# A vision transformer tower: q and k stacks of 128 rows with zeros, a shared tile for W1 and the k stack, and another interleaving of the two image streams

## What is computed

```
h = x_patches @ W + b, class token ahead, + position            # tokens, (64, 197, 192)
h = h + attention(norm(h))     # layer 0: one head of width 192
h = h + ffn(norm(h))           # layer 0: per image ONE of 3 experts, 192 -> 768 -> 192, gelu, scaled by its score
h = h + attention(norm(h))     # layer 1: 12 heads of width 16, scale 1/4, then a projection
h = h + ffn(norm(h))           # layer 1: 192 -> 768 -> 192 for the 191 tokens past the first six; the first six
                               # go through a routed pair of small networks, at the end of the kernel
```

## Time and profile before

| | |
|---|---|
| median of three runs | 4402.16 us (4379.66 to 4405.91) |
| profiled execution | 4418.51 us, span 4416.7 us |
| PE busy | 3398.2 us, 77%, 23190 matmuls |
| DVE busy | 2136.5 us, 48% |
| ACT busy | 1404.5 us, 32% |
| POOL busy | 361.6 us, 8% |
| mean granted TensorE clock | 0.805 of full speed |
| DMA | 284.55 MB, mean 64 GB/s |

### The profile page before, as it was taken

How to read it: one execution, slowest core, us unless ns; L and a number is a source line. 1 busy time by engine, 2 the same in 40 slices (tenths; PEclk the granted TensorE clock), 3 DMA queues, 4 the chain that set the end, 5 groups by cost and what they waited for, 6 DMA issues and landing times.

```text
span 4416.7 us, 63033 instructions
## 1 busy us (share of the span) xinstructions
PE 3398.2 (77%) x23190; PEld 3035.2 (69%) x23190; DVE 2136.5 (48%) x5286; ACT 1404.5 (32%) x2904; POOL 361.6 (8%) x746
## 2 busy tenths in 40 slices
PE   5778777777787777887777877777778777787767
PEld 4767776677776676776666777667677666677655
DVE  4454454545454445455444445444545545544433
ACT  2333333233333333333233333323333323233321
POOL 1010000000010001000001000000000000100000
PEclk8778888778887788787777787877888878778778
DMA  4332322233222233222233232223322223322222
GB/s 116 74 75 64 75 64 52 47 74 71 68 65 55 44 75 74 64 70 50 47 72 74 64 75 64 50 50 74 74 66 68 52 44 75 74 64 65 54 40 54
DMA packets 101366, 284.55 MB, mean 64 GB/s; under 512 B 24183, under 2 KB 65416, under 8 KB 90317
## 3 DMA queue, kind: packets, MB, share of 16 engines
q1 hardware_dynamic: 101324, 283.99, 28.3%
HBM read 189.87 MB, written 15.00 MB: 46 GB/s over the span
## 4 chain that ended last, share of the span: by engine, by line
PE 54%; DVE 22%; DMA 8%; issue 8%; ACT 3%; POOL 2%; SPq 1%; DVEq 0%; POOLq 0%; ACTq 0%
PE banks L634 24%; PE banks L678 10%; PE banks L777 6%; DMA stack<-low 6%; PE banks L810 4%; PE banks L796 4%; DVE inv L1052 4%; DVE hx L946 4%; PE banks L658 2%; DVE nmax L1041 2%; DVE stats L934 2%; DVE xnT L972 2%; POOL rstd L580 2%; DMA stack<-nmaxT 2%; ACT xnT L1182 1%
## 5 line engine op out<-in xcount | busy, mean ns | idle before, releaser
L777 PE MATMUL banks<-stack 64*99 64x198 f32 x1536 | 326.2, 383 | 325.9 <-issue 187.7
L777 PEld LDWEIGHTS banks<-stack 64*99 64x99 f32 x1536 | 270.6, 273 | 378.6 <-issue 208.3
L1041 DVE TENSOR_REDUCE nmax<-banks 99x4 f32<-99x788 f32 x384 | 358.1, 975 | 289.4 <-PE banks L777 289.4
L634 PE MATMUL banks<-xnT,fc_wT 128*128 128x198 f32 x1920 | 442.3, 419 | 42.1 <-DVE xnT L972 42.1
L634 PEld LDWEIGHTS banks<-xnT,fc_wT 128*128 128x128 f32 x1920 | 415.8, 328 | 60.9 <-DVE xnT L972 51.3
L1182 ACT ACTIVATE xnT<-banks 128x396 fp32r<-128x396 f32 x192 | 96.2, 501 | 946.9 <-PE banks L658 946.9
L796 PE MATMUL banks<-stack 65*99 65x198 f32 x1536 | 284.5, 316 | 120.0 <-DMA stack<-nmaxT 98.2
L578 POOL TENSOR_TENSOR var_eps<-moments,eps 99x2 f32<-99x2 f32 x256 | 51.6, 201 | 3890.3 <-DVE moments L939 3890.3
L678 PE MATMUL banks<-w_sb,hidT 128*99 128x192 f32 x1536 | 351.1, 394 | 0.0
L796 PEld LDWEIGHTS banks<-stack 65*99 65x99 f32 x1536 | 223.6, 212 | 178.1 <-issue 127.0
L946 DVE TENSOR_SCALAR hx<-hx,moments,rstd 99x192 f32<-99x192 f32 (+1 forms) x768 | 247.3, 384 | 161.4 <-POOL rstd L580 157.7
(11 more groups left out here) (188 smaller groups left out, 5453.9 us busy)
## 6 DMA issues: line engine op xcount, KB each, us to landing
w_sb<-w_split SPq DMA_DIRECT2D x64, 1536.0 KB
xin<-in_x_dram SPq DMA_DIRECT2D x32, 1176.0 KB
w_sb<-in_L_ffn_W_dram SPq DMA_DIRECT2D x64, 576.0 KB, 6.7
stack<-hi SPq DMA_DIRECT2D x64, 297.0 KB, 4.9
stack<-hi SPq DMA_DIRECT2D x128, 148.5 KB, 6.0
stack<-low SPq DMA_DIRECT2D x128, 148.5 KB, 7.0
stack<-low SPq DMA_DIRECT2D x64, 297.0 KB, 8.8
out_dram<-y SPq DMA_DIRECT2D x64, 73.5 KB
```

The source lines that it names most:

```text
L634: last = t_.matmul(dst, a, b, start=(j == 0), stop=(j == len(pairs) - 1))
L777: last = t_.matmul(b[n % 4][0:R, t * SP_:(t + 1) * SP_], stack[p][0:SLOT, block_of(n, 0), t * R:(t + 1) * R], stack[p][0:SLOT, block_of(n, ...
L1041: v.tensor_reduce(nmax1[p][:, :, 4 * j:4 * j + 2].rearrange("p t h -> p h t"), src, AX, ALU.max, negate=True).then_inc(nmax1_ready[p], 1)
```

## The change

Three things.

**128 rows.** The stack of one tile is split into `q_stack` and `k_stack`, 128 partitions each and twelve head blocks in natural order. The matmuls of `max` and `att` now take all 128 rows. Rows 64 to 127 of `q_stack` are set to zero once, at the start; the rows of `k_stack` hold whatever W1 left there, and meet zeros. Row 64 of `q_stack` gets the maxima in each image, so it is zeroed again by a small copy before the next image's `max` stages. The copies into the stacks are four for q, at qk1_0, and four for k, at qk1_1, instead of six at qk1_1; the maxima are placed by two copies.

**Places.** `q_stack` has a place of its own. The first three quarters of W1 and a little of the fourth share a tile (`shared`) with `k_stack`; W1's last quarter is a tile `w1_last`, which shares its place with `headT`. W1 is loaded in two pieces. To make room, the set-up that splits W1 into parts has two staging buffers instead of three.

**Order.** `MERGE` is another string.

```diff
-STAGED = 3
+STAGED = 2
-MERGE = ("bbbbbabbabbbbabbababbbabaababbbababaaabbaaabababararbaabrbabbbaabrbbarabbrbaaaaa"
-         "aaabaababaaaabaababaaabaaabbabbrabbabaabbab")
+MERGE = ("abababbbabbaaabbbbaababbababbbbaabbbbaaabaabrrabbraarbbbbaabbbraaaabbaabarababab"
+         "aaabaababaaabaaaaababrbaabbabbabbaabababbab")
...
+        q_stack = [sb(f"q_stack{p}", [128, HEADS, SP_], F32R) for p in range(2)]
...
-                    w1_sb.append(sb(f"w1_sb{p}", [128, 2, 2, F], F32R, weights))
-                stack.append(sb(f"stack{p}", [SLOT + 1, 2 * HEADS, SP_], F32R, loop))
+                w1_sb.append(shared[p][:, 0:3 * F].rearrange("p (a f) -> p a f", a=3))
+                k_stack.append(shared[p][:].rearrange("p (h s) -> p h s", h=HEADS))
+                with ExitStack() as heads:
+                    headT.append(sb(f"headT{p}", [128, GROUPS, SP_], stack=heads))
+                w1_last.append(sb(f"w1_last{p}", [128, F], F32R, loop))
...
-                if name == "qk1_1":
-                    sp.wait_ge(hi_ready[p], 2 * it + 2)
-                    q, k = slice(0, 2 * SP_), slice(2 * SP_, 4 * SP_)
...
-                    sp.dma_start(slots[p][0:HD], high).then_inc(stacked[p], 16)
-                    sp.dma_start(slots[p][HD:2 * HD, :, k], high[:, k]).then_inc(stacked[p], 16)
-                    sp.dma_start(slots[p][2 * HD:3 * HD, :, q], high[:, q]).then_inc(stacked[p], 16)
-                    sp.wait_ge(low_ready[p], 2 * it + 2)
-                    sp.dma_start(slots[p][HD:2 * HD, :, q], rest[:, q]).then_inc(stacked[p], 16)
-                    sp.dma_start(slots[p][2 * HD:3 * HD, :, k], rest[:, k]).then_inc(stacked[p], 16)
-                    sp.dma_start(slots[p][3 * HD:SLOT], rest).then_inc(stacked[p], 16)
+                if name in ("qk1_0", "qk1_1"):
+                    j = int(name[4])
+                    part = slice(2 * SP_ * j, 2 * SP_ * (j + 1))
...
+                    dst = (q_slots, k_slots)[j][p]
...
+                    sp.wait_ge(hi_ready[p], 2 * it + 1 + j)
+                    sp.dma_start(dst[0:HD], high).then_inc(stacked[p], 16)
+                    sp.dma_start(dst[(2 - j) * HD:(3 - j) * HD], high).then_inc(stacked[p], 16)
+                    if j == 0:
+                        sp.dma_start(q_stack[p][SLOT:SLOT + 1].bitcast(F32), q_stack[p][128 - HEADS:, 0, :].bitcast(F32)).then_inc(stacked[p], 16)
+                    sp.wait_ge(low_ready[p], 2 * it + 1 + j)
+                    sp.dma_start(dst[(1 + j) * HD:(2 + j) * HD], rest).then_inc(stacked[p], 16)
+                    sp.dma_start(dst[3 * HD:SLOT], rest).then_inc(stacked[p], 16)
                 if name == "maxT":
                     sp.wait_ge(nmaxT_ready[p], it + 1)
-                    sp.dma_start(stack[p][SLOT:SLOT + 1].bitcast(F32), nmaxT[p][:].bitcast(F32)).then_inc(nmax_placed[p], 16)
+                    sp.dma_start(q_stack[p][SLOT:SLOT + 1].bitcast(F32), nmaxT[p][0:HEADS].bitcast(F32)).then_inc(nmax_placed[p], 16)
+                    sp.dma_start(k_stack[p][SLOT:SLOT + 1].bitcast(F32), nmaxT[p][HEADS:].bitcast(F32)).then_inc(nmax_placed[p], 16)
...
-                                             stack[p][0:SLOT, block_of(n, 0), t * R:(t + 1) * R],
-                                             stack[p][0:SLOT, block_of(n, 1), :], start=True, stop=True)
+                                             q_stack[p][:, n, t * R:(t + 1) * R], k_stack[p][:, n, :], start=True, stop=True)
...
-                                             stack[p][:, block_of(s, 1), kt * R:(kt + 1) * R],
-                                             stack[p][:, block_of(s, 0), :], start=True, stop=True)
+                                             k_stack[p][:, s, kt * R:(kt + 1) * R], q_stack[p][:, s, :], start=True, stop=True)
...
+                v.memset(q_stack[p][SLOT:].bitcast(F32), 0.0)
```

More of the change, by code:

```diff
@@ L167, in two @@
                 return [sb(f"{name}{p}", shape, dt, stack) for p in range(2)]
-            w1_sb, stack = [], []
+            w1_sb, w1_last, k_stack, headT = [], [], [], []
+            shared = two("shared", [128, HEADS * SP_], F32R)
             for p in range(2):
-                with ExitStack() as weights:
-                    w1_sb.append(sb(f"w1_sb{p}", [128, 2, 2, F], F32R, weights))
-                stack.append(sb(f"stack{p}", [SLOT + 1, 2 * HEADS, SP_], F32R, loop))
-            slots = [stack[p][:].bitcast(F32).rearrange("k (h e) s -> k h (e s)", e=4) for p in range(2)]
+                w1_sb.append(shared[p][:, 0:3 * F].rearrange("p (a f) -> p a f", a=3))
[3 more added lines that the diff above has]
+                w1_last.append(sb(f"w1_last{p}", [128, F], F32R, loop))
+            k_slots, q_slots = [[s[p][:].bitcast(F32).rearrange("k (h e) s -> k h (e s)", e=2) for p in range(2)]
+                                for s in (k_stack, q_stack)]
             w2_sb = two("w2_sb", [128, HC, D])
@@ L227, in vit_kernel @@
             turned = [probs[p][0][:, 1, :, :] for p in range(2)]
-            headT = two("headT", [128, GROUPS, SP_])
             y = two("y", [R, T, D])
@@ L749, in stages @@
                     if name == "hid0_0":
-                        pe.wait_ge(w1_loaded[p], 48 * it + 48)
-                    hidden(p, 0, int(name[5]), w1_sb[p], lambda c: slice(c * 128, (c + 1) * 128))
+                        pe.wait_ge(w1_loaded[p], 64 * it + 64)
+                    hidden(p, 0, int(name[5]), lambda c: lambda part, k: w1_row(p, 2 * part + k)[:, c * 128:(c + 1) * 128])
                 elif name[:4] == "out0":
@@ L821, in stages @@
                     pe.wait_ge(xnT_ready[p], norm_count(4, it))
-                    hidden(p, 1, int(name[5]), fc1_wT, lambda c: slice(c * 128, (c + 1) * 128))
+                    hidden(p, 1, int(name[5]), lambda c: columns(fc1_wT, slice(c * 128, (c + 1) * 128)))
                 elif name[:4] == "out1":
@@ L875, in _ @@
             for p in range(2):
+                v.memset(q_stack[p][SLOT:].bitcast(F32), 0.0)
+            for p in range(2):
                 v.memset(probs0[p][:, :, SEQ:SP_], 0.0)
@@ L1040, in stages @@
                     src = banks[p][0:R, k:k + 2, 0:T * SP_].rearrange("p h (t s) -> p h t s", s=SP_)[:, :, :, 0:SEQ]
-                    v.tensor_reduce(nmax1[p][:, :, 4 * j:4 * j + 2].rearrange("p t h -> p h t"), src, AX, ALU.max,
+                    v.tensor_reduce(nmax1[p][:, :, 2 * j:2 * j + 2].rearrange("p t h -> p h t"), src, AX, ALU.max,
                                     negate=True).then_inc(nmax1_ready[p], 1)
```

25 lines of the change are left out of this document (14 added, 11 removed).

## The result

In one comparison on one chip the changed kernel took 4504.75 us (median of four runs, 4502.16 to 4512.26) and the kernel before 4400.51 us (four runs, 4379.66 to 4405.91): a ratio of 1.0249, 95% interval 1.0213 to 1.0284. The forecast was 4662. The direction and the range held; the size was 104 us instead of 260.

The account below looks back on a forecast made before the run. PE's instruction order bounds the kernel, through its stands and work at the 0.50 clock. Five segments gave +8.0 us per pair, +256 over 32 pairs, +260 with set-up: 4662 us, range 4360 to 4790.

Parts of the forecast that it names:

- the walk: PE's new order stepped through one image pair with the trace's durations: 137.8 us against 129.8.
- three signs of a wrong forecast: Period below 131 us, clock at 1.00 within 3 us of B's max0, or copies landing under 9 us.
- the zero rows at 0: Padding max and att matmuls to 128 rows: same matmuls and columns, taken as 0.
- the rival on the clock: 128 rows let the clock rise soon after each stand: 10 us per pair back, 4340 us; chance 0.15.
- the six steps: A's max steps with hid0_1, turn1, hid0_2 and out0_0 between: 11 us, most at the low clock.
- The order at +8.0 us per pair: The new order's large term, summed over one pair: 137.8 us against 129.8, +256 over 32 pairs.
- the segments: Five parts of a pair in PE's timeline: 8.7, 30.6, 26.5, 16.0 and 56.0 us forecast.
- the second: From A's qk1_0 to A's att0: 30.6 us against 25.6, PE standing about 11 us instead of 4.05.
- The first segment: From A's out0_1 to A's qk1_0: 8.7 us against 6.2, as B's turn2 and route now stand there.
- The copies at +0.8 and 0.6 us per pair: Stack copies: 0.8 us added for shorter pieces; the maxima's second copy: 0.6 us for one more issue.
- Set-up at +4 us: Two staging buffers instead of three make ScalarE wait for two landings more: 4 us, once.
- The tiling rule: Changing tiling mode drains TensorE, so padding would remove drains around max matmuls; evidence spoke against a large one.

Follow-up runs that it names:

- e4: The kernel before with only the new MERGE string (64 and 65 rows, one stack, six copies): 4879.33 us, ratio 1.1101 to the kernel before.
- e1: The changed kernel with only the old matmul rows back (64 in max, 65 in att): 4808.7 us, ratio 1.0943 to the kernel before.
- e3: The changed kernel with the old MERGE string and the old 64 and 65 rows, keeping new places and copies: 4256.96 us, ratio 0.9683 to the kernel before.
- e2: The changed kernel with only the old MERGE string back: 4171.19 us, ratio 0.9486 to the kernel before.
- e9: The changed kernel with the old MERGE string, except the new order up to A's qk1_0: 4173.18 us, ratio 0.9472 to the kernel before.
- e5: The changed kernel with 65 rows in att, still 128 in max: 4579.49 us, ratio 1.0390 to the kernel before.
- e7: The changed kernel with 96 rows in both max and att: 4607.8 us, ratio 1.0458 to the kernel before.
- e12: The changed kernel with the old MERGE string, B's out0_1 moved from ahead of A's max0 to between maxT and att0: 4276.38 us, ratio 0.9712.

## Where the prediction was right, and which step failed

**What bounds the kernel: right.** PE's order is the spine, and the stands ahead of max0 and the clock behind them are the two losses. (The 40 slices of the clock in the earlier trace rows lie between 0.72 and 0.90, not 0.7 and 0.8; nothing hangs on it.) In e4's profile 256 us of the order's price are stands and 199 PE at the lower clock (455; the medians differ by 485).

**Structures of the walk: right.** Forecast and found: 9 to 12 us ahead of A's max0, 10.70; 5 to 7 ahead of B's, 6.29; about 3 ahead of turn2 and route, 2.68 and 2.76; 3.7 ahead of A's att0, 3.37; stack copies at 110 to 125 GB/s, 123; 13 us for the stack, 13.05. None of the three signs of a wrong forecast came: the period is 133.1 and not under 131, the clock is back 8 us and not 3 after B's max0, the copies land after 13.05 and not 9 us.

**The step that failed: the zero rows at 0.** The prediction wrote "I take 0 for the matmul and let the walk set the clock, with about 6 us of closely packed work at 0.50 before it rises". The 6 us came from a stretch of 128-row work and were taken for every place, whatever its rows. They were not set against the 18.5 to 22 and 12.5 to 14.5 us that the same places took before with 64 and 65 rows, although the rival on the clock quoted the ends of just those two stretches. Measured, the rows are worth 304 us in the new order (e1) and 86 in the old (e3 to e2). The walk's period shows the same: its 137.8 us lie between e1's 142.3, with the old rows, and the changed kernel's 133.1.

The rival's price was 320 us, nearly the 304 measured. That is luck: it was read from the spells of the old order, where the rows are worth 86 us. And it was put as an alternative at 0.15 where it was a term that applies in every case. Its "against" was wrong in part: that VectorE sets the pace in the six steps holds for the max matmuls, but out0_0 and the later hid0 between them run at the restored clock.

**The order at +8.0 us per pair: stands right, clock missing.** With the old rows the order costs 485 us (e4), 15 per pair, of which 199 is slower work, since the walk gave the low clock about 6 us behind each stand. With 128 rows, for which 6 us was nearly true, it costs 334 us, all of it stands (347, and 17 less of work). Of the segments, those to A's qk1_0 (8.7 forecast, 9.5 measured), to A's att0 (30.6, 27.7), to B's max0 (26.5, 27.2), to B's att0 (16.0, 14.4) and to A's out0_1 end (56.0, 54.4) the second is off most. From A's max0 to att0 the walk had 15 us, with the six steps mostly at the low clock; they took 12.8, since the clock was back after 3.5. The first segment was right in length, but its piece alone costs 2 us (e9).

**The copies at +0.8 and 0.6 us per pair: wrong in sign.** Counted once per pair, that was +45 us, inside the 256. The new places and copies are worth -137 us in the old order and -71 in the new. The landing is indeed 0.8 us later from the first issue, but the q half is issued one stage earlier. In the old order the stands before max0 shrink by 0.8 and by 2 to 3.6 us. That the earlier q half does it was not tried by itself.

**Set-up at +4 us: right as a small term.** A's first qk1_0 starts at 143.26 us, before at 142.69: 0.6 us.

Put together from the kernel before: order +485, places and copies -71, and rows -304 give +110 (in the order e4, e1, after, each as measured), against +104 measured directly. The forecast had about +211 for the order, +45 for the copies and 0 for the rows. So the direction came out right in part by luck: with the rows at their measured 304 us and all else as forecast, the sum would have said faster. The order's price, too low, made up for it. The measured periods are 130.7 us before and 133.1 after (first to last of A's qk1_0, 31 pairs), +2.4 us where the sum said +8.0. The pair it was measured on, 129.8 us, was one of the shorter ones, which is 0.9 of the difference; the other 4.7 is the walk's.

**The tiling rule: not borne out.** The prediction weighed a sentence of the Trainium skill, "TensorEngine Tiling (Array Packing)", Key Properties, that a change of tiling mode drains TensorE. By it the padding would save drains, and 65, 96 and 128 rows would be alike. e5 and e7 are 75 and 103 us slower than 128 rows, and a max matmul takes 247 ns at best with 64 rows and 250 with 128. No run here shows a drain.

## What to carry to other kernels

Price a wait on TensorE as two terms, its length and the work behind it that runs at half clock, and read the second from the same place in the trace: here the order added 199 us of it to 256 us of stands with 64 rows (e4), and none to 347 with 128 (e2 to the changed kernel). A contraction over few rows can be worth padding with zeros next to such a wait, for the sake of the work around it; compare the windows behind it, since the padded matmul's own duration shows nothing. A stage moved to fill one wait can open another further on: look at what reads its result (e12). When a change bundles an order with other edits, run it once with the old order: here that gave a kernel 5.1% faster than before out of a change that as a whole was 2.5% slower.
